# First feed-forward with gate blocks first and 16-bit integers, expert rows found by 0/1 products and gathered

## The chip, the cores and the metric

One Trainium2 chip, one core. The time is the device time of one launch in microseconds; several launches of the same program are timed and the median is given. Beside them stands one execution under the hardware profiler, with its trace. The engines are TensorE (PE, its weight loads PEld), VectorE (DVE), ScalarE (ACT), GpSimd (POOL) and SyncE (SP), which here only issues DMAs; GpSimd's and SP's DMAs have queues of their own.

## The reference, cut to what matters

A residual stream `x` of 16 x 112 tokens (1792) and 256 features passes four stages: cross-attention, feed-forward, cross-attention, feed-forward. The change touches the two feed-forwards. In the first, every intermediate is rounded to integers of 16 bits with one scale for the whole tensor, so each scale needs the largest magnitude of all values:

```python
x = act_qdq(x)                              # act_qdq: round(x / s) * s, s = max|x| / 32767
up = act_qdq(x @ lpbq_dequant(w_up).T)      # 256 -> 768
gate = act_qdq(x @ lpbq_dequant(w_gate).T)
sig = fixed_qdq_u16(jax.nn.sigmoid(gate))   # round(s * 65536) / 65536, at most 65535 / 65536
gate = act_qdq(gate * sig)
o = act_qdq(gate * up)
return o @ lpbq_dequant(w_down).T           # 768 -> 256
```

The second is a mixture of experts: one shared expert for all tokens and 8 routed ones, of which each token uses its best 2 (hidden size 1024):

```python
shared = jnp.maximum(normed @ sw1 + sb1, 0.0) @ sw2 + sb2
probs = jax.nn.sigmoid(flat @ router_w.T)
scores, idx = jax.lax.top_k(probs, TOPK)
w = scores / (jnp.sum(scores, axis=-1, keepdims=True) + 1e-06)
comb = comb.at[jnp.arange(T)[:, None], idx].add(w)
h = jnp.maximum(jnp.einsum('td,edh->teh', flat, ew1) + eb1[None, :, :], 0.0)
eo = jnp.einsum('teh,eho->teo', h, ew2) + eb2[None, :, :]
routed = jnp.einsum('teo,te->to', eo, comb)
return shared + routed.reshape(b, s, -1)
```

## The kernel before, in words

The stages follow each other, each written as one block of five instruction lists, one an engine, that meet only at semaphores. All products are made of three float16 products (high by high, high by low, low by high), so most tensors exist as a high part, made by ScalarE, and a low part, made by VectorE.

**First feed-forward** (`feed_forward0_phase`). The tokens are four groups (`NG`) of 448 columns. For each group TensorE makes the six blocks (`OC0`) of 128 up rows and then the six of gate, 12 jobs of 6 matmuls; ScalarE copies each from PSUM into `U` or `G` (128 x 6 x 1792, float32), VectorE takes the largest magnitude of a group's six blocks (L774). When all 48 jobs are through, GpSimd reduces both maxima over the partitions (`partition_all_reduce`, L742), VectorE works out both scales (`scale_of`, L785). From there the work goes by the six blocks of 1792 columns: ScalarE rounds the gate by adding a large constant (L714), VectorE takes it away (L798), ScalarE makes the sigmoid and adds the constant again (`gate_sigmoid`), VectorE takes it away, multiplies and takes the maximum (`gated`, L754, L755, L757). GpSimd rounds `U` meanwhile (L747). After the second all-reduce ScalarE rounds the gated values in two passes (L722, L726) and VectorE multiplies by `U` and takes the maximum (L809, L812). After the third the output is rounded and split into float16 parts by groups (L734, L823), and TensorE makes the down products, which VectorE adds to `x_res` (L763).

**Second attention** (`attention1_phase`). SP loads the context of batch 0, then zeroes `slots_in`, a buffer in HBM of 35 x 128 rows of 265 numbers (L1041), then goes on with the contexts (L1032). It stores each finished `x` to `out`.

**MoE front** (`moe_front_phase`). It normalises the rows, transposes them, and computes the shared expert in 32 steps: step n makes hidden block n of 8 in token group n // 8 (`up`, 12 hidden products per block) and, three steps later (`LAG`), its part of the output (`second`, L1532). After every eighth step VectorE adds the group's output to the old `out` (`add`, L1644), which SP has loaded (`load_old`) and stores again (`store_new`); the next group's output uses the same PSUM, so its first `second` waits for that. In the same loop the 36 weight chunks of 512 KB, of the shared expert and of all eight experts, go through three staging buffers: SP loads, ScalarE writes the high part, VectorE the low part (`split`). `CHUNKS` says at which step which chunk is split. The list of VectorE is written out by hand: between `low(0)` and `low(9)` stand the pieces of the router. They rank each token in each expert by products with a triangular matrix, and give each of its two choices a slot in a table in which every expert begins at a multiple of 128. GpSimd then scatters the rows: 32 indirect DMAs (L1457), each of 112 rows of 265 numbers (row, token number, 8 shares), into `slots_in`. At steps 12 to 21 VectorE works out which expert a tile of 128 slots belongs to, and the tile's bias by eight pairs of operations (`bsel`, L1792).

**Expert tiles** (`routed_experts_phase`). For each of the 35 tiles (`MAXT`) SP loads 128 rows (L1844), TensorE transposes them, multiplies by the tile's expert, and GpSimd adds the result to `out` by an accumulating indirect DMA (L2002), whose indices and shares VectorE reads from the row (`read_row`). At most one of these is under way: the next waits for the one before.

## Time and profile before

| | us |
|---|---|
| median of 3 runs (lowest to highest) | 1815.92 (1814.92 to 1816.61) |
| profiled execution, its own time | 1819.4 |
| its span in the trace | 1817.6 |

Mean granted clock of TensorE: 0.892 of full speed. The span in 40 slices of 45.4 us, each digit the busy share of a slice in tenths:

```
PE   1799999999999945800738889889886665759997
DVE  6577767777777776487537889889887645545554
ACT  5466666666666634476327888888886524546664
POOL 4400001000000012020040000000000051002223
DMA  4110000000010010000060101101100233532321
```

By the trace the first feed-forward lies from 712 us to 898, the norm behind it to 921, the second attention to 1403, the MoE front to 1603.7, the expert tiles to 1804, and the end of the last scatter and the span's end follow. A slice stands for a share of time alone: which stage an engine's idle time lies in, and what ended it, are seen in the views by windows and in the timelines.

### The profile page before, as it was taken

Reading aid. Unit: us, or ns where it says so; the run is one execution under the profiler, and the core shown is the slowest. Engines: PE = TensorE matmul, PEld = TensorE weight load, DVE = VectorE, ACT = ScalarE, POOL = GpSimd, SP = SyncE. Lnnn points to the kernel's source line nnn. Section 1 sums busy time; section 2 is a strip of 40 time slices with the busy share of each in tenths; the row PEclk is TensorE's granted clock in tenths of the full one; section 3 lists DMA queues with packets and bytes.
Section 4 is the critical chain, followed back from the end, with each engine's and each line's share of the span. In section 5 each row is a group of like instructions: output and inputs, shape, how many; then the busy total and the mean of one; then the engine's idle time right before and its main releaser. Section 6 shows DMA issues by size and latency. Waiting matters only on the chain. (4 is left out here: it accounts for less than half of the span.)

```text
span 1817.6 us, 40958 instructions
## 1 busy us (share of the span) xinstructions
PE 1424.4 (78%) x15404; PEld 1011.8 (56%) x15404; DVE 1243.8 (68%) x3134; ACT 1138.0 (63%) x2422; POOL 220.1 (12%) x191
## 2 busy tenths in 40 slices
PE   1799999999999945800738889889886665759997
PEld 1566676667666633400725666666664434558885
DVE  6577767777777776487537889889887645545554
ACT  5466666666666634476327888888886524546664
POOL 4400001000000012020040000000000051002223
PEclk9899999999999987955857999999998677879999
DMA  4110000000010010000060101101100233532321
GB/s 143 36 36 18 19 19 24 30 18 19 19 36 10 2 53 1 0 0 0 22 140 16 31 16 31 31 17 31 31 11 21 90 124 120 173 91 44 51 48 25
DMA packets 46046, 74.80 MB, mean 41 GB/s; under 512 B 5689, under 2 KB 35106, under 8 KB 45858
## 3 DMA queue, kind: packets, MB, share of 16 engines
q1 hardware_dynamic: 39282, 64.74, 12.3%
q0 software_dynamic: 6576, 7.48, 2.5%
q8 instruction: 128, 2.10, 0.5%
q14 instruction: 60, 0.49, 0.1%
HBM read 50.16 MB, written 22.95 MB: 40 GB/s over the span
## 5 line engine op out<-in xcount | busy, mean ns | idle before, releaser
L519 ACT ACTIVATE a_pt<-a_ps_t 125x336 f16<-125x336 f32 x256 | 102.8, 449 | 107.5 <-PE a_ps_t L450 107.2
L1185 ACT ACTIVATE a_p<-a_s,a_nb 112x375 f32<-112x375 f32 x256 | 141.2, 599 | 28.4 <-DVE a_nb L1287 28.3
L291 PE MATMUL a_ps_o<-a_vh,a_pt 125*128 125x64 f16 (+1 forms) x1536 | 153.1, 183 | 3.3 <-ACT a_pt L1198 0.8
L293 PE MATMUL a_ps_o<-a_vh,a_pt 125*128 125x64 f16 (+1 forms) x1536 | 151.2, 182 | 0.0
L292 PE MATMUL a_ps_o<-a_vl,a_pt 125*128 125x64 f16 (+1 forms) x1536 | 151.1, 182 | 0.0
L1110 PE MATMUL a_ps_t<-ident,a_p 112*128 112x112 f32 x768 | 118.4, 284 | 41.6 <-ACT a_p L1185 40.6
L511 ACT ACTIVATE a_p<-a_ps_s,a_nb 112x375 f32<-112x375 f32 x256 | 144.1, 574 | 2.6 <-DVE a_scaled L591 2.6
L291 PEld LDWEIGHTS a_ps_o<-a_vh,a_pt 125*128 125x128 f16 x1536 | 133.5, 98 | 16.9 <-ACT a_pt L1198 8.4
L292 PEld LDWEIGHTS a_ps_o<-a_vl,a_pt 125*128 125x128 f16 x1536 | 131.0, 98 | 11.0 <-issue 0.2
L1287 DVE CUSTOM_DVE_ANT_0 a_s<-a_s,a_fill 112x375 f32<-112x375 f32 x256 | 130.0, 546 | 5.5
L1110 PEld LDWEIGHTS a_ps_t<-ident,a_p 112*128 112x128 f32 x768 | 79.7, 146 | 96.8 <-issue 81.0
L1278 DVE TENSOR_TENSOR a_s<-a_ps_s,a_mask 112x750 f32<-112x750 f32 x128 | 119.7, 935 | 20.1 <-PE a_ps_s L1100 15.0
L591 DVE TENSOR_SCALAR_CACHE_REDUCE a_scaled<-a_ps_s 112x375 f32<-112x375 f32 x256 | 129.0, 542 | 4.9 <-POOL x_res L544 3.6
L572 DVE TENSOR_TENSOR a_vl<-a_ps_j,a_vh 125x512 f16<-125x512 f32 x96 | 66.4, 692 | 93.2 <-ACT a_vh L495 93.2
L1922 ACT ACTIVATE e_h<-e_p,tile_b 128x128 f32<-128x128 f32 x280 | 87.0, 368 | 68.6 <-PE e_p L293 68.6
L293 PEld LDWEIGHTS a_ps_o<-a_vh,a_pt 125*128 125x128 f16 x1536 | 129.3, 97 | 0.0
L291 PE MATMUL a_ps_j<-a_cx,a_wk 128*128 128x375 f16 x320 | 106.4, 332 | 20.2 <-POOL a_neg L1223 10.7
L597 DVE TENSOR_TENSOR a_pt<-a_ps_t,a_pt 125x336 f16<-125x336 f32 x256 | 116.9, 498 | 1.1 <-ACT a_pt L519 1.0
L291 PE MATMUL a_ps_j<-a_wv,a_cx 128*125 128x512 f16 (+1 forms) x384 | 113.2, 312 | 2.6 <-DVE a_kl L1239 1.3
L293 PE MATMUL a_ps_j<-a_wv,a_cx 128*125 128x512 f16 (+1 forms) x384 | 112.0, 309 | 0.0
L292 PE MATMUL a_ps_j<-a_wv,a_cx 128*125 128x512 f16 (+1 forms) x384 | 112.0, 308 | 0.0
L291 PE MATMUL e_p<-e_xth,w1h 128*128 128x128 f16 x560 | 110.2, 222 | 1.8 <-DVE e_xtl L1948 1.8
(349 smaller groups left out, 4575.8 us busy)
## 6 DMA issues: line engine op xcount, KB each, us to landing
m_stage<-in_w SPq DMA_DIRECT2D x36, 512.0 KB
a_ctx<-in_ctxT SPq DMA_DIRECT2D x16, 375.0 KB, 3.6
ctx<-a_cx SPq DMA_DIRECT2D x16, 375.0 KB
a_cx<-ctx SPq DMA_DIRECT2D x16, 375.0 KB, 3.7
slots_in<-a_zeros SPq DMA_DIRECT2D x1, 4637.5 KB, 24.9
e_xt<-slots_in SPq DMA_DIRECT2D x35, 132.5 KB, 2.5
a_mask<-in_mask SPq DMA_DIRECT2D x16, 164.1 KB, 2.3
x_res<-in_x SPq DMA_DIRECT2D x1, 1792.0 KB, 11.0
```

The lines of the kernel that those rows point to most:

```text
L291: nc.tensor.matmul(out, wh, mh, start=(i == 0), stop=False)
L292: nc.tensor.matmul(out, wh, ml, start=False, stop=False)
L293: last = nc.tensor.matmul(out, wl, mh, start=False, stop=(i == n - 1))
L511: nc.scalar.activation(p32[:, g % 2, i, 0:NC], ps_s[0:S, i, 0:NC], ACT.Exp, bias=nb[:, g % 2, i:i + 1], scale=SC, accum_out=rsum[:, h:h + ...
L519: nc.scalar.activation(pt[:, g % 2, i, 0, :, 0:S], ps_t[0:KV, i, 0:NKV * S].rearrange("p (t s) -> p t s", t=NKV), ACT.Copy).then_inc(pt_hi, 1)
L591: nc.vector.tensor_scalar(scaled[:, i, :], ps_s[0:S, i, 0:NC], -SC, None, ALU.mult, ALU.min, accum_out=nb[:, g % 2, i:i + 1]).then_inc(max ...
L597: nc.vector.tensor_tensor(pt[:, g % 2, i, 1, :, 0:S], ps_t[0:KV, i, 0:NKV * S].rearrange("p (t s) -> p t s", t=NKV), pt[:, g % 2, i, 0, :, ...
L1110: mm = nc.tensor.matmul(ps_t[:, 2 * (g % 2) + i, t * S:(t + 1) * S], p32[:, g % 2, i, t * KV:t * KV + 128], ident32[0:S, 0:S], start=(t == ...
L1185: nc.scalar.activation(p32[:, g % 2, i, 0:NC], s2[:, g % 2, i, :], ACT.Exp, bias=nb[:, g % 2, i:i + 1], scale=-1.0).then_inc(exp_done, 1)
L1278: nc.vector.tensor_tensor(s1[:, r], ps_s[0:S, :, 0:NC], maskt[:, b % 2:b % 2 + 1, :].to_broadcast([S, 2, NC]), ALU.mult).then_inc(masked, 1)
L1287: nc.vector.tensor_tensor_reduce(out=s2[:, r, i, :], in0=s1[:, r, i, :], in1=fill[:, r, i, :], scale=-SC, scalar=3.0e38, op0=ALU.add, op1= ...
L1922: nc.scalar.activation(h32[:, 2 * (i % 2) + c, (j % 4) * 128:(j % 4 + 1) * 128], p1[:, 2 * (i % 2) + c, (j % 4) * 128:(j % 4 + 1) * 128], ...
```

## The change

**In the first feed-forward** all gate jobs are made before all up jobs. The scales of gate and up are reduced apart, so there are four all-reduces, and the rounding and sigmoids of the gate stand among ScalarE's copies of the up blocks. The integers are kept in tensors of 16-bit integers (the conversion rounds), so one operation rounds where two did; the high and low parts of the output lie in `U`. GpSimd's order is: reduce gate, reduce up, round six blocks of `U`, reduce gated, reduce output.

(The lines replaced are in the functions printed above; of them only a few are repeated here.)

```diff
+            for n in range(2 * NJ):
+                m, g, o = job(n)
+                w = (wgt, wup)[m]
+                wait(pe, copied, n - 5)
...
+            def round_gate(o):
+                if o == 0:
+                    act.wait_ge(scal, 1)
+                nc.scalar.activation(g_int[:, o, :], G[:, o, :], ACT.Copy, scale=sc[:, 2:3]).then_inc(g_rounded, 1)
...
+            def sigmoid(o):
+                act.wait_ge(g_rounded, o + 1)
+                wait(act, sig_rounded, o - 1)
+                nc.scalar.activation(sig[:, o % 2, :], g_int[:, o, :], ACT.Sigmoid, scale=sc[:, 3:4]
+                                     ).then_inc(sig_raw, 1)
...
+            for n in range(NJ + AHEAD):
+                take(n)
+            extra = [(f, o) for o in range(OC0) for f in (round_gate, sigmoid)]
+            for n in range(NJ + AHEAD, 2 * NJ):
+                take(n)
+                if extra:
+                    f, o = extra.pop(0)
+                    f(o)
+            for f, o in extra:
+                f(o)
...
-            act.wait_ge(scal, 2)
-            for o in range(OC0 + 1):
-                if o < OC0:
-                    nc.scalar.activation(G[:, o, :], G[:, o, :], ACT.Identity, bias=m_c[:], scale=sc[:, 5:6]
...
-                if o >= 1:
-                    act.wait_ge(g2_rounded, o)
-                    nc.scalar.activation(G[:, o - 1, :], G[:, o - 1, :], ACT.Identity, bias=m_neg[:]
...
+                nc.scalar.activation(g_int[:, o, :], G[:, o, :], ACT.Copy, scale=sc[:, 5:6]).then_inc(g2_rounded, 1)
+            act.wait_ge(scal, 4)
...
+                nc.scalar.activation(u_int[:, :, cc], G[:, :, cc], ACT.Copy, scale=sc[:, 7:8]).then_inc(o_rounded, 1)
                 act.wait_ge(o_rounded, g + 1)
-                nc.scalar.activation(oh[:, g, :, :], G[:, :, cc], ACT.Identity, bias=m_neg[:]).then_inc(o_hi, 1)
+                nc.scalar.activation(oh[:, g], u_int[:, :, cc], ACT.Copy).then_inc(o_hi, 1)
...
+            for n, c in enumerate((GATE, UP, GATED, OUT)):
                 pool.wait_ge(mx_part, n + 1)
...
-                nc.gpsimd.partition_all_reduce(am[:, c:c + k], mx[:, c:c + k], 128, bass.bass_isa.ReduceOp.max
+                nc.gpsimd.partition_all_reduce(am[:, c:c + 1], mx[:, c:c + 1], 128, bass.bass_isa.ReduceOp.max
...
+                if c == UP:
+                    pool.wait_ge(scal, 2)
                     for o in range(OC0):
-                        nc.gpsimd.tensor_scalar(U[:, o, :], U[:, o, :], sc[:, 1:2], MAGIC, ALU.mult, ALU.add
+                        nc.gpsimd.tensor_scalar(u_int[:, o, :], U[:, o, :], sc[:, 1:2], None, ALU.mult
...
+                nc.vector.tensor_scalar(sig_int[:, o % 2, :], sig[:, o % 2, :], UQ, UQ - 1.0, ALU.mult, ALU.min
+                                        ).then_inc(sig_rounded, 1)
+                dve.wait_ge(sig_rounded, o + 1)
+                nc.vector.tensor_tensor(G[:, o, :], sig_int[:, o % 2, :], g_int[:, o, :], ALU.mult).then_inc(gated, 1)
+                dve.wait_ge(gated, 2 * o + 1)
+                nc.vector.tensor_reduce(omx[:, 0, o:o + 1], G[:, o, :], AX.X, ALU.max, apply_absolute_value=True
+                                        ).then_inc(gated, 1)
+            def product(o):
+                dve.wait_ge(g2_rounded, o + 1)
+                dve.wait_ge(u_rounded, o + 1)
+                nc.vector.tensor_tensor(G[:, o, :], u_int[:, o, :], g_int[:, o, :], ALU.mult).then_inc(multiplied, 1)
+                dve.wait_ge(multiplied, 2 * o + 1)
+                nc.vector.tensor_reduce(omx[:, 1, o:o + 1], G[:, o, :], AX.X, ALU.max, apply_absolute_value=True
+                                        ).then_inc(multiplied, 1)
...
+            for n in range(NG):
+                largest(n)
+            largest_of_all(GATE)
...
+            dve.wait_ge(mx_all, 1)
+            link(scale_of(am[:, GATE:GATE + 1], sc[:, 0:1], sc[:, 3:4], sc[:, 2:3]))
             nc.vector.tensor_scalar(sc[:, 9:10], sc[:, 3:4], 1.0 / UQ, None, ALU.mult).then_inc(scal, 1)
...
+            largest(NG)
+            gated_product(0)
+            gated_product(1)
+            largest(NG + 1)
+            gated_product(2)
+            gated_product(3)
+            largest(NG + 2)
+            gated_product(4)
+            largest(NG + 3)
+            largest_of_all(UP)
+            gated_product(5)
             dve.wait_ge(mx_all, 2)
-            scale_of(am[:, 2:3], sc[:, 9:10], sc[:, 6:7], sc[:, 5:6])
+            scale_of(am[:, UP:UP + 1], sc[:, 0:1], sc[:, 4:5], sc[:, 1:2]).then_inc(scal, 1)
+            dve.wait_ge(gated, 2 * OC0)
+            nc.vector.tensor_reduce(mx[:, GATED:GATED + 1], omx[:, 0, :], AX.X, ALU.max).then_inc(mx_part, 1)
+            dve.wait_ge(scal, 2)
+            dve.wait_ge(mx_all, 3)
+            link(scale_of(am[:, GATED:GATED + 1], sc[:, 9:10], sc[:, 6:7], sc[:, 5:6]))
             nc.vector.tensor_tensor(sc[:, 10:11], sc[:, 6:7], sc[:, 4:5], ALU.mult).then_inc(scal, 1)
...
+                product(o)
...
+                nc.vector.tensor_tensor(ol[:, g], u_int[:, :, g * GW:(g + 1) * GW], oh[:, g], ALU.subtract
+                                        ).then_inc(o_split, 1)
```

**In the second attention** the zeroing of `slots_in` and its tensor of zeros are removed.

**In the MoE front** SP stores the 1792 normalised rows to HBM, in token order. VectorE splits each slot number into tile and row and writes 0/1 tensors, `at_row` (row in the tile, 128 wide) and `at_tile` (tile, 35 wide, three times: with the token number plus one and with both parts of the share); they lie in the memory of the normalised rows, so they wait for the store. TensorE's `find` multiplies them in 32 products, one a token group and choice, into a table of 35 columns that holds token and share of each slot of each tile. VectorE makes the indices from it, and GpSimd gathers the first three tiles. GpSimd also works out the biases of the tiles, in four operations, and adds the shared expert's output to `out` by accumulating DMAs; `out` is no longer loaded. All these stand in GpSimd's list in this order.

```diff
-            sp.wait_ge(zeros_made, 1)
-            sp.dma_start(xg.rearrange("(p r) d -> p r d", p=128),
-                         zeros[:].unsqueeze(1).to_broadcast([128, MAXT, ROW])).then_inc(cleared, 16)
...
-                sp.dma_start(x_old[:], out[g * TG:(g + 1) * TG].rearrange("t p d -> p t d")).then_inc(old_in, 16)
...
-                sp.wait_ge(added, TG * (g + 1))
-                sp.dma_start(out[g * TG:(g + 1) * TG].rearrange("t p d -> p t d"), x_old[:]).then_inc(stored, 16)
...
+                sp.dma_start(rows.rearrange("(t p) d -> p t d", p=S)[:, g * TG:(g + 1) * TG], norm[:, g * TG:(g + 1) * TG]
+                             ).then_inc(rows_out, 16)
 
             for c in range(NW):
+                if c in (3, 4):
+                    store_rows(2 * (c - 3))
+                    store_rows(2 * (c - 3) + 1)
                 wait(sp, w_lo, c - LB + 1)
...
-            for t in range(B):
-                for i in range(2):
-                    nc.gpsimd.indirect_dma_start(xg, bass.IndirectOffsetOnAxis(slot_idx[:, i, t:t + 1], 0),
-                                                 norm[:, t, :], None).then_inc(scattered, 16)
...
+            pool.wait_ge(rows_out, 16 * NG)
+            pool.wait_ge(index_ready, 1)
+            pool.wait_ge(located, 1)
+            for i in range(XR):
+                nc.gpsimd.indirect_dma_start(xt32[:, i, :], None, rows,
+                                             bass.IndirectOffsetOnAxis(pick[:, i:i + 1], 0)).then_inc(xt_in[i], 16)
+            def add_shared(g):
...
+                pool.wait_ge(added, TG * (g + 1))
+                nc.gpsimd.dma_start(out[g * TG:(g + 1) * TG].rearrange("t p d -> p t d"), y[:], accum_op=ALU.add
+                                    ).then_inc(stored, 16)
...
+            pool.wait_ge(tile_hot_ready, 1)
+            nc.gpsimd.tensor_tensor(bsel, tile_hot[:].unsqueeze(2).to_broadcast([128, MAXT, HC1, E]),
+                                    b1[:, 0:E, :].rearrange("p e j -> p j e").unsqueeze(1).to_broadcast(
+                                        [128, MAXT, HC1, E]), ALU.mult).then_inc(bias_made, 1)
+            for i, half in enumerate((4, 2, 1)):
+                pool.wait_ge(bias_made, i + 1)
+                nc.gpsimd.tensor_tensor(bsel[:, :, :, 0:half] if half > 1 else tile_b1[:].unsqueeze(3),
+                                        bsel[:, :, :, 0:half], bsel[:, :, :, half:2 * half], ALU.add
+                                        ).then_inc(bias_made, 1)
+            for g in range(NG):
+                add_shared(g)
...
+                pe.wait_ge(tiles_placed, 3)
+                for n in range(2 * B):
+                    pe.wait_ge(rows_placed, n // B + 1)
+                    mm = nc.tensor.matmul(px[:, 1, 0:3 * MAXT], at_row[:, n, :],
+                                          at_tile[:, n].rearrange("p a m -> p (a m)"), start=(n == 0),
+                                          stop=(n == 2 * B - 1))
+                mm.then_inc(located, 1)
...
+                if n == FIND_AT:
+                    find()
...
-                dve.wait_ge(old_in, 16 * (g + 1))
                 dve.wait_ge(down_done, g * HC1 + HC1)
+                wait(dve, stored, 16 * g)
...
-                    nc.vector.scalar_tensor_tensor(out=x_old[:, i, :], in0=p2[0:S, i, 0:D], scalar=gate[:],
-                                                   in1=x_old[:, i, :], op0=ALU.mult, op1=ALU.add).then_inc(added, 1)
+                    nc.vector.tensor_scalar(y[:, i, :], p2[0:S, i, 0:D], gate[:], None, ALU.mult).then_inc(added, 1)
...
-            nc.vector.tensor_copy(slot_idx[:], pos[:]).then_inc(slots_ready, 1)
...
             low(9)
+            dve.wait_ge(rows_out, 16 * NG)
+            dve.wait_ge(x_transposed, NG * KD)
+            dve.wait_ge(parts_ready, 1)
+            link(nc.vector.tensor_tensor(at_tile[:, :, 0], num_t[0:S].unsqueeze(1).to_broadcast([S, 2 * B, MAXT]),
+                                         pos_tile[:].rearrange("p i t -> p (i t)").unsqueeze(2).to_broadcast(
+                                             [S, 2 * B, MAXT]), ALU.is_equal))
+            for a, value in ((1, part16[:, 0]), (2, part16[:, 1]), (0, token[:])):
+                nc.vector.tensor_tensor(at_tile[:, :, a], at_tile[:, :, 0], value.rearrange("p i t -> p (i t)").unsqueeze(
+                    2).to_broadcast([S, 2 * B, MAXT]), ALU.mult).then_inc(tiles_placed, 1)
+            for i in range(2):
+                nc.vector.tensor_tensor(at_row[:, i * B:(i + 1) * B, :], lane[:].unsqueeze(1).to_broadcast([S, B, 128]),
+                                        pos_row[:, i, :].unsqueeze(2).to_broadcast([S, B, 128]), ALU.is_equal
+                                        ).then_inc(rows_placed, 1)
...
-                if n == 13:
...
+                if n == FIND_AT + 1:
+                    dve.wait_ge(located, 1)
+                    bias(nc.vector.tensor_copy(found_token[:], px[:, 1, 0:MAXT]))
...
+                    nc.vector.tensor_scalar(pick[:], found_token[:], -1.0, 0.0, ALU.add, ALU.max).then_inc(index_ready, 1)
...
+                    nc.vector.scalar_tensor_tensor(out=target[:], in0=found_token[:], scalar=-1.0, in1=unfilled[:],
+                                                   op0=ALU.add, op1=ALU.add)
...
-                if 14 <= n < 14 + HC1:
-                    bias(nc.vector.tensor_tensor(bsel[:], tile_hot[:],
-                                                 b1[:, 0:E, n - 14].unsqueeze(1).to_broadcast([128, MAXT, E]),
-                                                 ALU.mult))
-                    bias(nc.vector.tensor_reduce(tile_b1[:, :, n - 14], bsel[:], AX.X, ALU.add))
```

**In the expert tiles** GpSimd gathers each tile's rows by index, five tiles ahead of the result it next scatters; `read_row` is gone, and shares and indices come from the table.

```diff
-            for i in range(MAXT):
-                wait(sp, x_transposed, i - XR + 1)
-                wait(sp, row_read, i - XR + 1)
-                sp.dma_start(xt32[:, i % XR, :], xg[i * 128:(i + 1) * 128, :]).then_inc(xt_in[i % XR], 16)
...
         def _(pool):
+            def gather(i):
+                pool.wait_ge(x_transposed, i - XR + 1)
+                nc.gpsimd.indirect_dma_start(xt32[:, i % XR, :], None, rows,
+                                             bass.IndirectOffsetOnAxis(pick[:, i:i + 1], 0)).then_inc(xt_in[i % XR], 16)
+            for i in range(XR, XR + LAG):
+                gather(i)
             for i in range(MAXT):
+                if i + XR + LAG < MAXT:
+                    gather(i + XR + LAG)
                 pool.wait_ge(y_ready, i + 1)
```

## Rows read from the trace of the kernel before

**Rows 1.** The page, part 1: busy us (share of the span) x instructions
```profile
PE 1424.4 (78%) x15404; PEld 1011.8 (56%) x15404; DVE 1243.8 (68%) x3134; ACT 1138.0 (63%) x2422; POOL 220.1 (12%) x191
```

**Rows 2.** Windows: us; busy (x instructions) PE, PEld, DVE, ACT, POOL; PE clock, DMA share, GB/s
```profile
712.00:768.00 56.00, 54.64 (x288) 28.11 (x288) 21.24 (x10) 26.15 (x48) 0.00 (x0) 1.00 0.00 0
...
768.00:854.00 86.00, 0.00 (x0) 0.00 (x0) 71.08 (x60) 54.22 (x31) 14.14 (x9) 0.52 0.00 0
...
854.00:898.00 44.00, 34.34 (x288) 33.65 (x288) 19.61 (x24) 20.34 (x8) 0.00 (x0) 0.85 0.00 1
...
1470.00:1512.00 42.00, 15.72 (x73) 9.32 (x73) 7.00 (x11) 4.50 (x6) 28.10 (x30) 0.64 0.40 124
...
1536.00:1567.00 31.00, 23.68 (x156) 17.50 (x156) 19.10 (x27) 17.77 (x24) 0.00 (x0) 0.89 0.52 165
...
1700.00:1800.00 100.00, 100.00 (x1205) 81.12 (x1203) 52.30 (x146) 65.02 (x199) 27.82 (x18) 1.00 0.26 43
```

**Rows 3.** Timeline of VectorE, feed-forward: start us, us, engine line op out<-in [idle before]
```profile
767.52 2.95 DVE L774 TENSOR_REDUCE f_gmx<-f_G  x1 [3.83 <-ACT f_G L710]
...
804.62 1.08 DVE L754 TENSOR_SCALAR f_sig<-f_sig 128x1792 f32<-128x1792 f32 x1
...
807.80 2.02 DVE L757 TENSOR_REDUCE f_omx<-f_G 128x1 f32<-128x1792 f32 x1
...
828.39 2.03 DVE L809 SCALAR_TENSOR_TENSOR f_G<-f_U,f_G 128x1792 f32<-128x1792 f32 x1 [5.40 <-ACT f_G L726]
...
859.53 2.96 DVE L823 SCALAR_TENSOR_TENSOR f_ol<-f_G,f_oh 128x2688 f16<-128x2688 f32 x1 [5.26 <-ACT f_oh L734]
```

**Rows 4.** Timeline of ScalarE, feed-forward: the rounding of the gate (two merged)
```profile
773.14 3.65 ACT L714 ACTIVATE f_G<-f_G,f_mc,f_sc 128x1792 f32<-128x1792 f32 x2 [5.78 <-DVE f_sc L795]
```

**Rows 5.** Timeline of GpSimd, feed-forward with the norm before it
```profile
700.36 8.25 POOL L912 TENSOR_TENSOR qw_q<-qw_q,qw_bscale 128x1536 f32<-128x1536 f32 x3 [6.82 <-issue]
...
770.81 0.38 POOL L742 PARTITION_ALL_REDUCE f_am<-f_mx  x1 [62.20 <-DVE f_mx L778]
...
778.25 13.03 POOL L747 TENSOR_SCALAR f_U<-f_U,f_sc 128x1792 f32<-128x1792 f32 x6 [7.06 <-issue]
```

**Rows 6.** Timeline of TensorE and of SP's queue, start of the second attention
```profile
954.14 0.47 PE L291 MATMUL a_ps_j<-a_cx,a_wk 128*128 128x375 f16 x1 [5.82 <-DMA a_cx<-ctx]
...
928.49 0.60 SPq L1041 DMA_DIRECT2D slots_in<-a_zeros  x1
...
929.14 12.50 SPq L1032 DMA_DIRECT2D a_cx<-ctx  x1
```

**Rows 7.** Timeline of GpSimd, MoE front: first and last of 32 scatters
```profile
1466.46 1.57 POOL L1457 DMA_INDIRECT slots_in<-x_res,m_slot_idx  x1 [58.79 <-issue]
...
1505.99 0.94 POOL L1457 DMA_INDIRECT slots_in<-x_res,m_slot_idx  x1 [0.30 <-issue]
```

**Rows 8.** Timeline of TensorE, MoE front: restarts and one of the pauses
```profile
1477.45 0.68 PE L1532 MATMUL m_p<-w,m_hh 128*112 128x256 f16 x2 [5.26 <-DVE m_x_old L1644]
...
1507.87 0.37 PE L1532 MATMUL m_p<-w,m_hh 128*112 128x256 f16 x1 [2.43 <-issue]
...
1536.58 0.68 PE L1532 MATMUL m_p<-w,m_hh 128*112 128x256 f16 x2 [8.56 <-DVE m_x_old L1644]
...
1567.64 0.67 PE L1532 MATMUL m_p<-w,m_hh 128*112 128x256 f16 x2 [7.38 <-DVE m_x_old L1644]
```

**Rows 9.** Timeline of VectorE, MoE front: a comparison with broadcast operands
```profile
1491.06 0.41 DVE L1792 TENSOR_TENSOR m_bsel<-m_num_t,m_ends 128x245 f32<-128x245 f32 x1
```

**Rows 10.** Waits of SP's queue, MoE front: us in total, times, longest
```profile
SPq L1417 <- DMA out_x<-m_x_old: 15.6, 3, 5.9
```

**Rows 11.** Timeline of SP and TensorE at the start of the expert tiles
```profile
1603.67 5.80 SPq L1844 DMA_DIRECT2D e_xt<-slots_in  x4
...
1607.24 0.68 PE L1863 MATMUL e_px<-ident,e_xt 128*128 128x128 f32 x2 [20.74 <-issue]
```

**Rows 12.** The tile e_y (accumulating scatter of the expert tiles), landing
```profile
DMA to landing us min/median/max: 2.7/3.8/5.2
```

346 lines of the change are left out of this document (146 added, 200 removed).

## The prediction

> **What bounds the kernel now.** I read the busy shares first: TensorE is busiest, yet only 78% [rows 1], so the time lies in stages with different limits. The table of windows shows them [rows 2]. In the first feed-forward TensorE works from 712 to 768 and then stands from 768 to 854: 86 us in which VectorE, ScalarE and GpSimd pass the same tensors around. It works again from 854 to 898. In the last stage (the 35 expert tiles) TensorE is busy 100 of 100 us at clock 1.00, 5.5 us a tile; nothing that relieves another engine helps there. The stage before it, the MoE front, is the odd one: from 1470 to 1512 TensorE is busy 15.7 of 42 us, ScalarE 4.5 and VectorE 7.0. Nobody works, and the DMA engines are at a share of 0.40.
>
> The timeline of that stretch says why. GpSimd issues 32 scatters, one each 1.25 us, from 1466.5 to 1506.9 [rows 7]. In the same time TensorE's matmuls come one at a time, each after mostly 1.5 to 3.5 us of "issue", which means that the engine waited for no semaphore and no data; the row of 1507.87 stands for eleven such [rows 8]. Pauses end with the scatters: from 1512 it runs at full pace. I read it as TensorE not getting its instructions while the row-wise packets fill the DMA engines. From the first restart after a group, 1477.45, to the next, 1536.58, one group of eight hidden blocks takes 59.1 us; the next group, to 1567.64, takes 31.1 [rows 8].
>
> **The change, part 1: first feed-forward.** Gate jobs go first. 48 jobs take 54.6 us of TensorE [rows 2], 1.14 each, so the gate half ends at 712.0 + 27.4 = 739.4. Last copy 0.6 (48 take 26.2 us of ScalarE) and last maximum 2.95: 743.0. From that point to the scales it takes 2.7 us now (770.47 to 773.14, [rows 3, 4]); one of two scales is left, so 1.9: 744.9 instead of 773.1.
>
> From there VectorE is the longest queue. Six tiles, each a scaling of the sigmoid (1.08), a multiply (as the product of 2.03) and a maximum (2.02, [rows 3]), make 5.2 each, 31 us; the four maxima of the up blocks now stand between them, 4 x 2.95 = 11.8. ScalarE alternates a copy (0.6) with a rounding or sigmoid (3.65 for two, [rows 4]), 2.4 a pair, so the first sigmoid arrives only at 751, and TensorE's second half, paced by these copies, ends at 778 instead of 766; I give 5.5 us of waits. VectorE is through at 744.9 + 31 + 11.8 + 5.5 = 793.2; now it is 821.4. That is 28 us earlier.
>
> Most of it is then lost in GpSimd's queue. It now reduces the up maximum, rounds six tiles of U, and only then reduces the gated maximum, for which all wait. Before, the rounding (13.0 us for six, 2.2 each where it meets VectorE, 1.75 otherwise) lay under the sigmoids [rows 5]; its cover is gone. And after an all-reduce the next ordinary operation of GpSimd starts 7.06 and 6.82 us later, for "issue", at both places where it occurs [rows 5], though one had its scale 5 us before. So a switch of kind costs about 7 us. Up all-reduce done at 788.5, rounding from 795.5, 6 x 1.75 = 10.5: 806. The way back to an all-reduce is always under idle time in this trace: bounds 0 and 7.06. I take 7, by the other direction. 813, plus 0.4 and 1.0 for the scales: 814.4 against 823.0. Gain 8.6. The Trainium skill, "GPSIMD Engine Reference", section "Instruction dispatch", says that the first call to a freshly loaded kernel pays about 6 us of loading, with no visible instruction. That speaks against this order; with its 6 us both ways this stage would gain 2 us more, and the two pauses of the trace bear it out in one direction.
>
> After that scale the first product now waits 5.40 us, for ScalarE to add and take away the rounding constant in two passes [rows 3]; with integers one pass of 1.9 does. Gain 3.4. The six products and maxima stay VectorE's (4.0 a tile). The last 44 us are TensorE's (34.3 busy) behind two ScalarE passes and one low part of 2.96 [rows 3]. The low part now has three 16-bit operands; no row shows such an operation, so it lies between 0 and 1.5 us less, and I take 0 by the row of the same shape. The Trainium skill, "VectorE: DVE Perf Modes", section "The perf-mode tier table", gives a tensor_tensor of 16-bit operands twice the rate; it would make the sum 1.4 us better, and no row here has that form. Part 1: 8.6 + 3.4 = 12 us.
>
> **Part 2: no zeroing of the slot rows.** It is queued on SP at 928.5 ahead of the second batch's context, whose load then issues for 12.5 us; TensorE waits 5.82 us for it at 954 [rows 6]. Gone, with 0.3 us of memset. 6 us; bounds 0 (VectorE paces those slots anyway) and 8.
>
> **Part 3: MoE front.** The 32 scatters go, and with them the pauses. What a group costs without them: TensorE busy 23.7 us [rows 2] and the hand-over at its end, 7.4 where the weight chunk came late, 5.3 where it did not [rows 8]. SP's late chunks come from its waits for the old output, 15.6 us in three [rows 10]; these go too, since y is now added by GpSimd's accumulating DMA. So 29 us a group. The first carries the 32 products of find(), 105 columns each, 2.5 us between the transposes and the 256-column matmuls. It also carries the first accumulation: GpSimd must gather three tiles (1.25 each), build the biases (4200 elements in four operations at the 1.8 ns of the multiply of 1536 elements in [rows 5]: 8 us) and then issue; y is one buffer, so the second add may wait: 2 us, bounds 0 and 6. Group 1: 59.1 - 33.5 = 25.6. Group 2: 31.1 - 29 = 2.1. Last part, now 1567.6 to 1603.7: 4 less without SP's wait, the last accumulation landing later than a plain store.
>
> Against it stands new VectorE work at one point, between low(9) and low(10): four operations of 1120 elements and two of 2048. By 0.41 us for 245 elements [rows 9] and 2.02 for 1792, that is 4 x 1.3 + 2 x 2.3 = 9.8 us. Behind it are low(10), split(7), low(11), split(8) and add(0), for which TensorE waits already; I count 7.4 us of it (bounds 0 and 9.8). The scalings and stores of rows (1.8 MB on SP, early) meet chunks that are needed 10 us later: nothing; were that cover gone, 5 us. The bias selection that leaves VectorE was beside other work. Part 3: 25.6 + 2.1 + 4 - 7.4 = 24.3.
>
> **Part 4: expert tiles.** TensorE's first transpose starts 3.6 us after the block, behind the load of x [rows 11]; the gathers are made before it. It has five registers to load still: 2 us. Afterwards GpSimd issues a scatter (1.55) and a gather (0.94) in a tile of 5.5 us, ahead by two tiles: nothing.
>
> **Sum.** 12 + 6 + 24.3 + 2 = 44.3 us, against the profiled execution: 1819.4 - 44.3 = 1775. That one stood 3.5 above the median of 1815.9, so the median should come to **1771**.
>
> **Rivals.**
> (a) The pauses are not the scatters' but the weights', or the gathers and accumulating DMAs bring them back. For it: the weights load at the same time. Against: at 1536 to 1567 they load faster, 165 GB/s against 124, with no pause [rows 2]. Then part 3 is 2.1 + 4 - 7.4, and the time 1815.9 - 19 = 1797.
> (b) GpSimd's way back is free and the new VectorE block is half hidden: 7 + 3.7 better, 1760. For it: the return was never seen to cost. Against: the pauses after both all-reduces are of one length.
> (c) Slower. In the expert stage the gather now shares GpSimd's queue with the accumulating scatter, which lands in 3.8 us [rows 12]. If a pair holds the queue longer than a tile's 5.5 us, every tile waits; from 6.8 us on (44.3 / 35 more) the whole gain is gone, and at 7.5 the time is 1816 - 44 + 70 = 1842. Against: 32 scatters were issued and drained in 46 us, 1.4 each, so a pair takes 2.9.
> (d) The 16-bit forms are slower than the 32-bit ones (scaling of the sigmoid at 2.02, not 1.08: 5.6 us; rounding at 2.2: 2.5 us) and each of three hand-overs waits 4 us for the accumulation (12, of which 2 are counted): 1816 - 44 + 18 = 1790. For it: no row has such a form. Against: it takes all of them together.
>
> **Chances.** Forecast 0.57, (a) 0.12, (b) 0.17, (c) 0.03, (d) 0.11. Best case of all bounds: 21 + 8 + 36 + 4 = 69, 1747; (d) and (a) close the range above. I give 1747 to 1796. A measurement of this kernel tells 0.2% (3.6 us) from no change: faster 0.95, within 0.01, slower 0.04.
>
> **What would show it.** After: gate scale at 745; GpSimd's six roundings back to back from 795 and a gap of about 7 us before the third all-reduce, which the first wait of the products ends; feed-forward end near 885. No wait for the context at the start of the second attention. No "issue" pauses of TensorE in the front, DVE products of 9.8 us in one block, group restarts 29 to 34 us apart, front shorter by 24. Tiles still 5.5 us. Wrong if TensorE still crawls in the front, if the tiles grow, or if the third all-reduce comes before 800.

## The result and the profile after

The changed kernel takes 1801.49 us (median of 5 runs, 1796.12 to 1808.35), the kernel before, run beside it, 1815.92. The ratio is 0.9927, 95% interval 0.9900 to 0.9954; a second comparison on another occasion (after_again, below) gave 0.9915, 0.9900 to 0.9929. So the change is worth 13 to 15 us, where 45 were predicted and the range ended at 1796. Its profiled execution, 1800.8 us with a span of 1799.0, lies at its median; the one of before lay 3.5 above its own.

The spans differ by 18.6 us. Cut at points that both traces show (the last addition to `x_res` in the feed-forward; TensorE's first transpose in the MoE front; the restarts after a group of eight hidden blocks; the first transpose of the expert tiles), the difference is made up so:

| stretch | before | after | difference | predicted |
|---|---|---|---|---|
| to the end of the first feed-forward | 897.4 | 899.4 | +2.0 | -12 |
| norm, second attention, start of the front | 520.6 | 508.9 | -11.7 | -6 |
| first transpose to first restart | 59.4 | 65.1 | +5.7 | +7.4 |
| first to second restart | 59.1 | 43.6 | -15.5 | -25.6 |
| second to third restart | 31.1 | 29.4 | -1.7 | -2.1 |
| third restart to first expert transpose | 39.6 | 39.7 | +0.1 | -6 |
| from there to the end | 210.4 | 212.9 | +2.5 | 0 |

Three lines carry the miss: the feed-forward (14 us), the first group of steps (10) and the passage to the expert tiles (6). The attention gave back 6 of them, and the last line's 2.5 comes back under "Open". The profiled execution of after_again differs from that of before, in the same order, by +3.1, -6.7, +3.7, -15.4, -1.6, -0.5 and +2.6 us: what differs from one execution of the changed kernel to the other is the attention, not the three lines.

The page of the changed kernel, part 1, to be read against [rows 1]: GpSimd alone has become clearly busier, by 41 us.

```profile
PE 1423.2 (79%) x15436; PEld 1012.5 (56%) x15436; DVE 1228.2 (68%) x3022; ACT 1111.6 (62%) x2410; POOL 261.3 (15%) x203
```

The timeline of GpSimd in the feed-forward, which answers to [rows 5]:

```profile
743.93 0.38 POOL L738 PARTITION_ALL_REDUCE f_am<-f_mx  x1 [34.96 <-DVE f_mx L758]
786.82 1.11 POOL L738 PARTITION_ALL_REDUCE f_am<-f_mx  x1 [42.51 <-DVE f_mx L758]
794.86 28.70 POOL L743 TENSOR_SCALAR f_ui<-f_U,f_sc 128x1792 int16<-128x1792 f32 x6 [6.93 <-issue]
829.74 0.38 POOL L738 PARTITION_ALL_REDUCE f_am<-f_mx  x1 [6.19 <-issue]
```

The order of events is the predicted one: two all-reduces, a pause, six roundings, a pause, the third all-reduce. What differs is one duration: 28.70 us for six roundings, 4.78 each, where the same number of elements took 2.2 with a float32 result [rows 5]. VectorE stood still the whole time, so this is GpSimd by itself. VectorE's timeline says what that costs (compare [rows 3]):

```profile
792.40 0.15 DVE L813 TENSOR_REDUCE f_mx<-f_omx 128x1 f32<-128x6 f32 x1
830.23 0.16 DVE L762 TENSOR_TENSOR f_sc<-f_am,f_sc 128x1 f32<-128x1 f32 x1 [37.67 <-POOL f_am L738]
...
833.01 2.03 DVE L780 TENSOR_TENSOR f_G<-f_ui,f_gi 128x1792 f32<-128x1792 int16 x1 [1.85 <-ACT f_gi L726]
...
863.91 1.56 DVE L829 TENSOR_TENSOR f_U<-f_ui,f_U 128x2688 f16<-128x2688 int16 x1 [5.15 <-ACT f_U L732]
```

VectorE was through with the gated maxima at 792.6 (793.2 predicted, 821.5 before) and then stood for 37.67 us, released by GpSimd's all-reduce. The first product waits 1.85 us for ScalarE where it waited 5.40, and the low part takes 1.56 for 2.96.

In the MoE front, TensorE's restarts (compare [rows 8]) and VectorE around them:

```profile
1473.47 0.68 PE L1565 MATMUL m_p<-w,m_hh 128*112 128x256 f16 x2 [9.90 <-DVE m_y L1679]
...
1517.05 0.68 PE L1565 MATMUL m_p<-w,m_hh 128*112 128x256 f16 x2 [18.31 <-DVE m_y L1679]
...
1546.40 0.68 PE L1565 MATMUL m_p<-w,m_hh 128*112 128x256 f16 x2 [5.26 <-DVE m_y L1679]
```

```profile
1463.95 4.49 DVE L1830 TENSOR_TENSOR x_res<-m_lane,m_pos_row 112x2048 f16<-112x2048 f16 x2
...
1489.09 1.27 DVE L1660 SCALAR_TENSOR_TENSOR w1l<-m_stage,m_nws,w1h 128x1024 f16<-128x1024 f32 x1
...
1491.40 6.82 DVE L1660 SCALAR_TENSOR_TENSOR w1l<-m_stage,m_nws,w1h 128x1024 f16<-128x1024 f32 x1 [0.41 <-ACT w1h L1597]
1498.14 2.97 DVE L1672 TENSOR_TENSOR m_hl<-m_h,m_hh 128x448 f16<-128x448 f32 x1
...
1515.33 1.66 DVE L1679 TENSOR_SCALAR m_y<-m_p,m_gate 112x256 f32<-112x256 f32 x4 [8.27 <-DMA out_x<-m_y]
```

No issue pause is left between the restarts. But one split (L1660) takes 6.82 us and the next low part 2.97, for 1.28 and 0.63; and at the second hand-over VectorE waits 8.27 us for the accumulation of the first output, which TensorE sees as 18.31. GpSimd's timeline of the same time holds both causes:

```profile
1489.70 1.49 POOL L1462 DMA_INDIRECT x_res<-normed_rows,tile_pick  x1 [0.30 <-issue]
1491.21 5.92 POOL L1470 TENSOR_TENSOR x_res<-m_tile_hot,m_b 128x2240 f32<-128x2240 f32 x1
1497.21 4.88 POOL L1475 TENSOR_TENSOR x_res<-x_res 128x1120 f32<-128x1120 f32 x2
1502.17 1.55 POOL L1475 TENSOR_TENSOR tile_b<-x_res 128x280 f32<-128x280 f32 x1
1503.67 1.38 POOL L1466 DMA_DIRECT2D out_x<-m_y  x1
```

The bias operations run from 1491.2 to 1503.7, and the slow split starts 0.2 us after the first of them and ends 1.1 us after it. The accumulation, whose data were ready at 1473.4, is issued behind them, and it lands only 11.6 us later, at 1515.2; the three after it take 5.3 to 5.5.

### The profile page after: what moved, and what is told of

Its sections match the earlier page's. It is cut to its first block and busy times, and to the rows that moved or that the text cites. A ratio compares the mean times of both kernels' runs of the same rounds, so it can differ in the third digit from the quotient of the medians.

```text
span 1799.0 us, 40612 instructions
## 1 busy us (share of the span) xinstructions
PE 1423.2 (79%) x15436; PEld 1012.5 (56%) x15436; DVE 1228.2 (68%) x3022; ACT 1111.6 (62%) x2410; POOL 261.3 (15%) x203
## 5 line engine op out<-in xcount | busy, mean ns | idle before, releaser
L2003 DVE TENSOR_TENSOR e_hl<-e_h,e_hh 128x512 f16<-128x512 f32 x70 | 48.5, 693 | 101.7 <-ACT e_hh L1978 101.7
```

## The experiments

All were timed in 5 rounds beside the kernel before; times are medians, ratios those to before in the same rounds. Theory A: the feed-forward's gain is held back in GpSimd's list; theory C: GpSimd's bias operations slow VectorE and hold back the accumulation. Their rivals B and D are told with the runs.

### The feed-forward: u_on_scalar, u_float_on_gpsimd, ff_alone

**u_on_scalar** takes the six roundings off GpSimd:

```diff
-                    pool.wait_ge(scal, 2)
-                    for o in range(OC0):
-                        nc.gpsimd.tensor_scalar(u_int[:, o, :], U[:, o, :], sc[:, 1:2], None, ALU.mult
-                                                ).then_inc(u_rounded, 1)
...
-            act.wait_ge(scal, 3)
+            act.wait_ge(scal, 2)
             for o in range(OC0):
+                nc.scalar.activation(u_int[:, o, :], U[:, o, :], ACT.Copy, scale=sc[:, 1:2]).then_inc(u_rounded, 1)
+                if o == 0:
+                    act.wait_ge(scal, 3)
                 nc.scalar.activation(g_int[:, o, :], G[:, o, :], ACT.Copy, scale=sc[:, 5:6]).then_inc(g2_rounded, 1)
```

> The changed kernel with the six roundings of U moved from GpSimd to ScalarE (one ahead of the third scale, the others in turn with the gated roundings). Theory A, GpSimd's list held the third all-reduce back by 37 us (pause 6.9, six int16 roundings 28.7, pause 6.2): the all-reduce comes about 1 us after VectorE's last maximum, near 793; a rounding takes 1.8 us on ScalarE; the feed-forward ends near 864 and not 899, and the time falls by 35 to about 1766. Rival B, the third all-reduce is late for its own sake (another all-reduce, or the pauses of GpSimd, whatever lies between): it comes after 800 and the time is 1780 or more.

Measured: 1766.45 us, ratio 0.9721 (0.9700 to 0.9743). The timelines of GpSimd, of ScalarE and of VectorE in its trace:

```profile
787.58 1.11 POOL L741 PARTITION_ALL_REDUCE f_am<-f_mx  x1 [42.51 <-DVE f_mx L758]
793.40 0.35 POOL L741 PARTITION_ALL_REDUCE f_am<-f_mx  x1 [4.71 <-DVE f_mx L813]
```

```profile
793.27 1.79 ACT L726 ACTIVATE f_ui<-f_U,f_sc 128x1792 int16<-128x1792 f32 x1 [14.03 <-DVE f_sc L765]
```

```profile
796.77 2.03 DVE L780 TENSOR_TENSOR f_G<-f_ui,f_gi 128x1792 f32<-128x1792 int16 x1 [1.98 <-ACT f_gi L729]
```

The third all-reduce comes at 793.4, 5.8 us after the second and with no pause between: two of a kind needed none here. The first product starts at 796.8 for 833.0, and the feed-forward ends at 863.0. Theory A holds to the size; rival B fell. One edit is worth 35 us, more than twice what the whole change brought.

**u_float_on_gpsimd** leaves the roundings where they are and gives them the old float32 form:

```diff
-                        nc.gpsimd.tensor_scalar(u_int[:, o, :], U[:, o, :], sc[:, 1:2], None, ALU.mult
+                        nc.gpsimd.tensor_scalar(U[:, o, :], U[:, o, :], sc[:, 1:2], MAGIC, ALU.mult, ALU.add
...
-                nc.vector.tensor_tensor(G[:, o, :], u_int[:, o, :], g_int[:, o, :], ALU.mult).then_inc(multiplied, 1)
+                nc.vector.scalar_tensor_tensor(out=G[:, o, :], in0=U[:, o, :], scalar=-MAGIC, in1=g_int[:, o, :],
+                                               op0=ALU.add, op1=ALU.mult).then_inc(multiplied, 1)
```

> The changed kernel with U rounded in float32 again (multiply, add the large constant, in place) on GpSimd at the same point of its list; VectorE takes the constant away in the product. If the 16-bit result is what makes a rounding 4.78 us: six roundings take 10.5 to 13 us, both pauses stay, the third all-reduce comes at 812 to 814 as predicted, and the time is 1801 - 17 = 1784. If the place in the list or the memory makes them slow: 28.7 us again and 1801.

Measured: 1783.79 us, ratio 0.9814 (0.9792 to 0.9836). GpSimd's timeline:

```profile
794.05 10.42 POOL L743 TENSOR_SCALAR f_U<-f_U,f_sc 128x1792 f32<-128x1792 f32 x6 [6.99 <-issue]
810.23 0.38 POOL L738 PARTITION_ALL_REDUCE f_am<-f_mx  x1 [5.76 <-issue]
```

This is the prediction's own chain, almost row for row: 10.42 us of roundings (10.5 predicted), a pause each way. Neither the place in the list nor the pauses make the difference, but the form of the operation: 1.74 us against 4.78 for 1792 elements. With the type the destination changes too (`U` in place, or `u_int`), and no run separates the two; ScalarE writes the same tensor `u_int` in 1.79 us in u_on_scalar.

**ff_alone** is the kernel before with the new `feed_forward0_phase`.

> The kernel before with the first feed-forward of the change alone. Theory A: that part costs 2 us (its end at 899.4 against 897.4), so 1816 to 1819, no difference that can be told. If the missing gain lay in the expert part alone, the feed-forward's predicted 12 us would show here: 1804.

Measured: 1818.66 us, ratio 1.0012 (0.9999 to 1.0024). The part that was to bring 12 us brings nothing or costs 2, as its trace (end at 899.2) and that of the changed kernel say.

### The zeroing: zero_late

The kernel before, with the zeroing queued behind batch 3's context:

```diff
-            sp.wait_ge(zeros_made, 1)
-            sp.dma_start(xg.rearrange("(p r) d -> p r d", p=128),
-                         zeros[:].unsqueeze(1).to_broadcast([128, MAXT, ROW])).then_inc(cleared, 16)
...
                 load(b)
+                if b == 3:
+                    sp.wait_ge(zeros_made, 1)
+                    sp.dma_start(xg.rearrange("(p r) d -> p r d", p=128),
+                                 zeros[:].unsqueeze(1).to_broadcast([128, MAXT, ROW])).then_inc(cleared, 16)
```

> The kernel before with the zeroing of the slot rows queued on SP behind the load of batch 3's context and not ahead of batch 1's. If the zeroing's place is what costs: no wait of 5.8 us for the context near 954, later work 5 us earlier, 1816 - 6 = 1810. Rival: the wait is only moved, since the next context (or a store of x) then waits for the 24.9 us of zeroing: 1816.

Measured: 1811.85 us, ratio 0.9959 (0.9946 to 0.9972), so 5 to 10 us. TensorE at the place of [rows 6]:

```profile
947.92 0.49 PE L291 MATMUL a_ps_j<-a_cx,a_wk 128*128 128x375 f16 x1 [0.26 <-DVE a_vl L1255]
```

The wait is gone, not moved. What the table calls 11.7 us is in part the spread between executions: from the feed-forward's end to the front's first transpose the profiled executions of the six kernels here that zero early take 516.8 to 521.4 us, nine of kernels with no zeroing at all 508.5 to 515.0, with means 7.3 us apart; the changed kernel's first one lies at the low end. The prediction's 6 is within what can be told from this.

### The front: bias_on_vector, y_two_buffers, table_spread

**bias_on_vector** removes GpSimd's four operations and puts back VectorE's eight pairs:

```diff
-            nc.gpsimd.tensor_tensor(bsel, tile_hot[:].unsqueeze(2).to_broadcast([128, MAXT, HC1, E]),
...
+                if 16 <= n < 16 + HC1:
+                    bias(nc.vector.tensor_tensor(bsel, tile_hot[:],
+                                                 b1[:, 0:E, n - 16].unsqueeze(1).to_broadcast([128, MAXT, E]),
+                                                 ALU.mult))
+                    bias(nc.vector.tensor_reduce(tile_b1[:, :, n - 16], bsel, AX.X, ALU.add))
```

> The changed kernel with the biases of the tiles worked out on VectorE at steps 16 to 23 by eight pairs of operations, as before, and not on GpSimd. Theory C, GpSimd's four large operations slow VectorE down (a split of 6.82 us for 1.28 while they run) and hold back the first accumulation: splits take 1.28, the first accumulation is issued near 1492, no wait for it at the next hand-over, the first group takes 33 to 35 us for 43.4, and the time is 1801 - 9 = 1792. Rival D, the gathers or the weight chunks slow VectorE: the splits stay slow and the time stays at 1801.

Measured: 1789.79 us, ratio 0.9853 (0.9829 to 0.9876). The timelines of GpSimd, of VectorE and of TensorE:

```profile
1493.66 1.41 POOL L1465 DMA_DIRECT2D out_x<-m_y  x1
```

```profile
1493.88 1.28 DVE L1651 SCALAR_TENSOR_TENSOR w1l<-m_stage,m_nws,w1h 128x1024 f16<-128x1024 f32 x1 [0.42 <-ACT w1h L1588]
```

```profile
1475.95 0.67 PE L1556 MATMUL m_p<-w,m_hh 128*112 128x256 f16 x2 [9.90 <-DVE m_y L1670]
1506.74 0.68 PE L1556 MATMUL m_p<-w,m_hh 128*112 128x256 f16 x2 [5.53 <-DVE m_y L1670]
```

The split that took 6.82 takes 1.28 at the same place, though gathers and weight chunks are what they were (rival D fell), and the group takes 30.8 us for 43.6. The kernel gains 12 us although VectorE has more to do.

**y_two_buffers** leaves the biases on GpSimd and alternates between `m_y` and a free part of the row memory, each with a semaphore of its own:

```diff
-        y = sb("m_y", [S, TG, D])
+        y = (sb("m_y", [S, TG, D])[:], x_all[0:S, B - TG:B, :])
...
-                wait(dve, stored, 16 * g)
+                wait(dve, stored[g % 2], 16 * (g // 2))
```

> The changed kernel with two buffers for the shared expert's output, so that VectorE waits only for the accumulation before the last. If the wait of 8.3 us at the second hand-over is on the path: first group 43.4 - 8 = 35, 1793. Rival: the hand-over then waits for TensorE instead and 3 us are left of it: 1798.

Measured: 1792.63 us, ratio 0.9859 (0.9838 to 0.9880); the group takes 35.2 us (1471.84 to 1507.03). The slow split is still 6.82 us there. So of the 12.8 us that bias_on_vector wins in the group, 8.4 are the late accumulation, and the other 4.4, by subtraction, come with VectorE's slow operations.

**table_spread** is bias_on_vector with the six table operations handed out one a step, from step 11 on; `find` moves from step 12 to 17, the bias pairs from 16 to 20, and the first accumulation is issued ahead of the gathers:

```diff
+            places = [place_tile, lambda: place_value(1, part16[:, 0]), lambda: place_value(2, part16[:, 1]),
+                      lambda: place_value(0, token[:]), lambda: place_row(0), lambda: place_row(1)]
...
+                if n >= 11 and places:
+                    places.pop(0)()
```

> bias_on_vector (1790) with VectorE's six table operations set one each into steps 11 to 16 and not in a block of 9.5 us ahead of step 10, the find at step 17, the first accumulation issued ahead of the gathers. If the block is on the path at its full length, as the trace suggests (the first restart 5.3 us later than before, where 7.4 was forecast): first restart 9 us earlier, 2 us lost again in the steps that take the operations, 1783. Rival: the steps are bound by VectorE, so that all 9.5 us come back: 1790.

Measured: 1795.6 us, ratio 0.9869 (0.9849 to 0.9890): no gain over 0.9853. The first restart comes 59.3 us after the first transpose and not 65.1, but the group behind it takes 37.65 and not 30.8 (1475.67 to 1513.32). One of its steps on VectorE:

```profile
1491.48 1.28 DVE L1653 SCALAR_TENSOR_TENSOR w1l<-m_stage,m_nws,w1h 128x1024 f16<-128x1024 f32 x1
1492.68 2.28 DVE L1827 TENSOR_TENSOR x_res<-m_lane,m_pos_row 112x2048 f16<-112x2048 f16 x1
1494.88 0.62 DVE L1665 TENSOR_TENSOR m_hl<-m_h,m_hh 128x448 f16<-128x448 f32 x1
```

No idle time stands in brackets: VectorE works without a gap through these steps. A step passes ScalarE in 2.45 us, and low part and split take 1.9 of it on VectorE, so it has half a microsecond a step to give, not 2.3. That is the rival's account. The trace has a second cost beside it, which the place of `find` brings: at step 17 TensorE itself waits for the last two of these operations, 4.1 us together, and ScalarE then stands 7.78 us for TensorE:

```profile
1495.11 0.95 PE L1528 MATMUL m_px<-x_res 112*128 112x105 f16 x16 [1.23 <-DVE x_res L1827]
1498.96 1.59 PE L1528 MATMUL m_px<-x_res 112*128 112x105 f16 x16 [2.90 <-DVE x_res L1827]
```

The group grows by 6.9 us, and these waits are in it. A spread table with a later `find` was not tried, so the run doesn't show that spreading can't pay.

### TensorE's pauses: no_scatters, scatters_of_eight, scatters_spaced, plain_copies

Each is the kernel before with only the scatters of `moe_front_phase` altered. **no_scatters** leaves them out, so the routed experts see empty rows and add nothing:

```diff
-                    nc.gpsimd.indirect_dma_start(xg, bass.IndirectOffsetOnAxis(slot_idx[:, i, t:t + 1], 0),
-                                                 norm[:, t, :], None).then_inc(scattered, 16)
```

> The kernel before without its 32 scatters of rows (the slot rows stay zero, so the routed experts add nothing to the output). If TensorE's pauses in the front are the scatters', as the prediction has it: no matmul after an issue pause between the first and second restart, that group of steps takes 33 us for 59, and the time is 1816 - 26 = 1790. Rival (a), the weights' loading makes them: pauses stay and 1816.

Measured: 1790.05 us, ratio 0.9851 (0.9838 to 0.9864); the first group takes 31.9 us (1475.12 to 1506.98) for 59.1. The predicted size holds, and the scatters are the cause; the first half of rival (a), the weights, fell.

**scatters_of_eight** cuts each to 8 rows, so most tokens are not given to the experts:

```diff
-                    nc.gpsimd.indirect_dma_start(xg, bass.IndirectOffsetOnAxis(slot_idx[:, i, t:t + 1], 0),
-                                                 norm[:, t, :], None).then_inc(scattered, 16)
+                    nc.gpsimd.indirect_dma_start(xg, bass.IndirectOffsetOnAxis(slot_idx[0:8, i, t:t + 1], 0),
+                                                 norm[0:8, t, :], None).then_inc(scattered, 16)
```

> The kernel before with scatters of 8 rows each in place of 112, 32 of them as before (the routed experts then see few tokens). If the number of row packets is what stops TensorE's and ScalarE's instructions from coming: pauses gone, 1790 as without scatters. If each scatter does, whatever its size (its issue on GpSimd, 1.25 us, and what goes with it): pauses stay, the group takes 55 us or more, 1812 to 1816.

Measured: 1816.24 us, ratio 1.0000 (0.9987 to 1.0012). The first theory of the two fell, and with it the prediction's reading of the pauses. **plain_copies** issues 32 DMAs of the same 112 rows to fixed places, so the experts see other tokens' rows:

```diff
-                    nc.gpsimd.indirect_dma_start(xg, bass.IndirectOffsetOnAxis(slot_idx[:, i, t:t + 1], 0),
-                                                 norm[:, t, :], None).then_inc(scattered, 16)
+                    n = (i * B + t) * S
+                    nc.gpsimd.dma_start(xg[n:n + S, :], norm[:, t, :]).then_inc(scattered, 16)
```

> The kernel before with 32 plain DMAs issued by GpSimd back to back, each 112 rows to a fixed place in the slot rows and not to computed rows (the routed experts see tokens of other experts). If the computed indices are what stops the other engines: no pauses, 1790. If any DMA that GpSimd issues does: the group takes 55 us or more and the time stays at 1816.

Measured: 1791.35 us, ratio 0.9866 (0.9844 to 0.9889). The windows 1470 to 1512 of scatters_of_eight and of plain_copies (columns as in [rows 2], where the kernel before has 15.72 us of TensorE, 0.40 and 124 GB/s):

```profile
1470.00:1512.00 42.00, 15.95 (x71) 9.61 (x70) 6.12 (x10) 5.73 (x9) 25.01 (x29) 0.63 0.15 43
```

```profile
1470.00:1512.00 42.00, 29.25 (x180) 21.21 (x179) 27.41 (x45) 19.64 (x27) 12.31 (x24) 0.84 0.78 221
```

In the first, TensorE starves at a DMA share of 0.15; in the second it works at 0.78. Traffic is not it, and neither is every DMA that GpSimd issues: it takes the ones with computed row numbers, whatever they carry. One thing changes along with the row numbers: GpSimd issues the 32 plain DMAs in 16.9 us, the 32 of eight rows in 38 and those of before in 40.5, so the runs don't separate the row numbers from GpSimd's longer work on each.

**scatters_spaced** keeps them whole and makes each wait for a step:

```diff
                 for i in range(2):
+                    pool.wait_ge(h_lo, 10 + (2 * t + i) * 21 // 32)
                     nc.gpsimd.indirect_dma_start(xg, bass.IndirectOffsetOnAxis(slot_idx[:, i, t:t + 1], 0),
```

> The kernel before with the 32 scatters spread over steps 10 to 30 of the loop, one or two a step and not back to back. If a scatter's issue on GpSimd stops the others' instructions for a fixed time each: 27 us are lost all the same, over three groups of steps, and the time stays at 1816. If only a dense row of them does (a queue that fills), as in the expert stage, where one every 5.5 us leaves TensorE busy 100 of 100 us: no pauses, near 1790.

Measured: 1796.1 us, ratio 0.9883 (0.9862 to 0.9904). The groups take 33.2, 34.0 and 41.2 us to the first expert transpose, 108.5 together; before it was 129.8, without scatters 102.8. So the same scatters cost 27 us back to back and 6 when spread over the steps: a dense row of them is what starves the engines. Neither pure theory holds; the second is near. By this, 20 us of what the gather was built for could be had with one line.

### Together: all_mended, last_add_late, after_again

**all_mended** takes u_on_scalar, table_spread with the biases on VectorE, and a wait for the accumulations by the first expert scatter in place of SP's at the front's end:

```diff
-            sp.wait_ge(stored, 16 * NG)
...
                 pool.wait_ge(y_ready, i + 1)
+                if i == 0:
+                    pool.wait_ge(stored, 16 * NG)
```

> The changed kernel with all repairs: U rounded on ScalarE (35 us), biases on VectorE (11.7), the table operations spread over steps (6 to 7), and the accumulations awaited by GpSimd ahead of its first expert scatter and not at the end of the front (3). If they add up: 1801.5 - 35 - 11.7 - 6.5 - 3 = 1745. If they compete (the clock, VectorE's steps): 1752 or more.

Measured: 1755.52 us, ratio 0.9651 (0.9634 to 0.9669), short of the sum by what the spread table and the moved wait did not bring: the third restart to the first expert transpose is 39.3 us for 39.7. Nothing in the front waits for the last accumulation any more, yet the front ends behind it: the last split ends at 1534.8, the accumulation lands at 1537.3, and TensorE's first instruction of the expert stage comes at 1538.0.

**last_add_late** leaves the table block whole, and moves the last accumulation itself into the expert stage:

```diff
-            for g in range(NG):
+            for g in range(NG - 1):
                 add_shared(g)
...
+            nc.gpsimd.dma_start(out[(NG - 1) * TG:NG * TG].rearrange("t p d -> p t d"), y_shared[:], accum_op=ALU.add
+                                ).then_inc(stored, 16)
             for i in range(XR, XR + LAG):
                 gather(i)
```

> The changed kernel with U rounded on ScalarE, the biases on VectorE, the table block left whole, and the last accumulation of the shared output issued as GpSimd's first work of the expert stage, awaited by its first scatter. If the end of the front waits until GpSimd's own last DMA has landed (6.8 us from VectorE's last split to TensorE's first transpose for 3.8 before, whoever waits for it): these 3 us come back, and with 35 and 11.7 the ratio to before is 0.963, 1750. If the 3 us are something else's: first transpose still 6.8 us after the last split, 1753.

Measured: 1751.47 us, ratio 0.9637 (0.9625 to 0.9650), 3.6% below before and 2.8% below the change. The timelines of GpSimd, of VectorE and of TensorE at the passage:

```profile
1532.20 1.19 POOL L2035 DMA_DIRECT2D out_x<-y_shared  x1 [31.75 <-POOLq L1329]
```

```profile
1530.20 1.23 DVE L1649 SCALAR_TENSOR_TENSOR w<-m_stage,w 128x1024 f16<-128x1024 f32 x1 [1.12 <-ACT w L1586]
```

```profile
1536.62 0.69 PE L1909 MATMUL e_px<-ident,x_res 128*128 128x128 f32 x2 [17.71 <-issue]
```

From the last split's end, 1531.4, to the first transpose it is 5.2 us, for 6.9 in the changed kernel (1579.2 to 1586.1) and 3.8 before. What fills these stretches, apart from the wait for the landing, are five loads of a register from `tile_expert`, with which TensorE opens the stage: before, in the changed kernel, and here (durations in ns, minimum, median and maximum, then first and last start):

```profile
L1849 PEldq TENSOR_LOAD <-tile_expert x5: 295/309/487, 1603.8 to 1606.6; - x5
L1898 PEldq TENSOR_LOAD <-tile_expert x5: 297/309/491, 1582.6 to 1585.5; - x5
L1895 PEldq TENSOR_LOAD <-tile_expert x5: 311/490/1197, 1531.8 to 1535.1; - x5
```

From the last split's end to the first of these loads it is 0.4 us before, 3.4 in the changed kernel and 0.4 here: the accumulation's landing did hold the front's end, and its 3 us came back. Of them 1.3 were lost again, since two of the loads are slow here (0.68 and 1.20 us); no run shows why.

**after_again** is the changed kernel once more.

> The changed kernel unaltered, on the chip and in the rounds of the three others: 0.992 to 0.993 of before, 1802, front and tail as in its first profile (the last 28 us from the last transpose on, where before takes 25.5).

Measured: 1801.3 us, ratio 0.9915 (0.9900 to 0.9929).

## Why the prediction was wrong

**Part 1, 14 us.** "6 x 1.75 = 10.5" for the six roundings is the step that failed. Everything around it held: VectorE through at 792.6 (793.2), start of the roundings 794.9 (795.5), the way back 6.19 us (7, "bounds 0 and 7.06"), which settles the first half of rival (b): the way back is not free. The 28.70 us put the third all-reduce at 829.7, not 813. Rival (d) had the right doubt, that no row showed a 16-bit form, and priced it at 2.2 us a rounding; an upper bound from a row of the same operation with another result type was no bound. On VectorE and ScalarE the forms cost nothing (1.09, 2.02, 1.78 us). Against that the first product gained 3.5 (3.4 predicted), and the end 2.6 where 0 was taken: mostly the low part, 1.56 us for 2.96. The Trainium skill's "VectorE: DVE Perf Modes", section "The perf-mode tier table", gives a tensor_tensor of 16-bit data twice the rate, and the trace agrees for this one with 16-bit inputs and result; the product with a float32 result stays at 2.02. The pauses lie on both sides of the roundings, 6.9 and 6.2 us; by the Trainium skill, "GPSIMD Engine Reference", section "Instruction dispatch", the first call to a freshly loaded kernel pays about 6. If each change of kind is such a first call, the trace agrees in both directions; that it is one, no run shows.

**Part 2.** The term held: 6 us forecast, 7.5 by zero_late (5 to 10), 7.3 between the means of the two sets of kernels. The table's 11.7 and after_again's 6.7 are two executions of one kernel, and what the table shows beyond the forecast is luck of the one execution.

**Part 3, 10 us in the first group.** "59.1 - 33.5" had the scatters right (no_scatters: 31.9 us for the first group) and failed at what takes their place. GpSimd's bias operations were costed in its own queue only ("8 us", measured 12.4), and not against VectorE, whose list they stopped: shown by bias_on_vector. And "y is one buffer, so the second add may wait: 2 us, bounds 0 and 6" measured 8.3, because the accumulation is queued behind gathers and biases (issued at 1503.7, in bias_on_vector at 1493.7) and lands 11.6 us after its issue (9.8 there); that this wait is on the path is shown by y_two_buffers. The group comes out as 33.5 + 6.3 for the wait + 4.4 for the slow operations = 44.2, for 43.6 measured. The Trainium skill's page "SBUF — State Buffer", section "SBUF: two separate sides", describes the port pair that VectorE and GpSimd share as an exclusive lock: an instruction of GpSimd, or one of VectorE with two inputs from SBUF or in a two-port mode, has it for its whole length if it starts first. The rows agree, down to the split that ends 1.1 us after GpSimd's 5.92 us operation. I had weighed no row for this, though the trace of before shows it from VectorE's side, while GpSimd rounds `U` (778.3 to 791.3, [rows 5]) and after it:

```profile
784.46 3.46 DVE L755 TENSOR_TENSOR f_G<-f_sig,f_G 128x1792 f32<-128x1792 f32 x1
793.26 2.02 DVE L755 TENSOR_TENSOR f_G<-f_sig,f_G 128x1792 f32<-128x1792 f32 x1
```

The same multiply takes 3.46 us beside a rounding and 2.02 alone, and the rounding 2.2 there and 1.74 alone in u_float_on_gpsimd. The prediction read the second of these ("2.2 each where it meets VectorE") and did not ask the same of VectorE.

**The table block** was put at 7.4 us on the path: 5.7 by the table, 3 to 6 over the seven kernels that have it (62.4 to 65.1 us to the first restart, 59.1 to 60.3 without). Its whole length, 9.5 us, was estimated at 9.8. This is between the forecast and rival (b)'s second half.

**The last part and part 4, 6 us.** The splits did end 3.0 us earlier (32.8 us from the third restart, for 35.8), of 4 forecast. But the front's end now waits until the last accumulation has landed, 3.0 us more than before, whoever waits for it (all_mended); the prediction named that landing and gave it no price. And Part 4's "2 us" rests on a misreading: the first transpose was not "behind the load of x". That load has landed at 1605.8, and TensorE's register loads end at 1607.2, right before the transpose at 1607.24; in [rows 11] the transpose has "issue" for its wait and not the load. They take 3.5 us before and in the changed kernel, so removing the load brought nothing.

**Rivals.** (a) fell: the pauses are the scatters', and 35 gathers, three in the front and 32 a tile apart, bring none back. That its 1797, itself just outside the range given, lies nearest to the 1801 measured is luck. (c) fell: a scatter and a gather take 1.59 and 0.99 us of 5.5, and 34 tiles take 184.6 us for 184.9. Of (d), the roundings came, at seven times its 2.5 us; the sigmoid's scaling did not (1.09), and of three hand-overs one waited for the accumulation. The price of the pauses was right by the wrong mechanism: "the row-wise packets fill the DMA engines" is refuted by scatters_of_eight and plain_copies.

**Open.** By what path 32 indirect DMAs keep instructions from TensorE and ScalarE is not shown; only that rows and bytes don't matter, and that density and the indirect form (or GpSimd's longer work on it) do. And from the issue of the last expert scatter to the end it takes 7.3 us in the kernels with gathers and 4.7 in those without; nothing was tried on these 2.6 us, which are the last line of the table.

## What to carry to other kernels

Price an operation with a new result type only by a row of that type on that engine; if there is none, test it alone before building on it, and keep it off a queue for which the others wait. An operation moved to an engine with spare time is to be costed twice, in that engine's list (what is queued behind it, and each change between all-reduce and ordinary work) and against VectorE, whose operations it can hold up. And where many small indirect DMAs are issued in a row, spreading them may bring most of what removing them would.

## What the runs showed of the hardware that was not expected

- GpSimd's multiply of 1792 float32 elements with an int16 result: 4.78 us; with a float32 result in place, a second operation included, 1.74.
- A GpSimd tensor_tensor of 2240 elements (5.92 us) beside VectorE's split of 1.28 us made that 6.82 us.
- The front's block does not end before GpSimd's last DMA has landed, though nothing in it waits for that DMA (all_mended): 3 us.
- 32 back-to-back indirect DMAs of 8 rows cost TensorE 27 us, 32 plain ones of 112 rows nothing that can be told from leaving them out (0.9866 and 0.9851); spread over 21 steps, the indirect ones of 112 rows cost 6.
